# One core of Trainium2: the step products of a linear-attention layer, with s split 1 + 3 groups instead of 2 + 2

## The reference

```
for i in range(12):
    q, k, v = split(x @ Wqkv[i].T + bqkv[i])            # 16 heads of 8
    att = (q @ k.T) * scale                              # per head, no softmax
    x = (att @ v) @ Wproj[i].T + bproj[i] + x
x = layernorm(x0 + x)
x = layernorm(x + (silu(x @ wg.T) * (x @ wu.T)) @ wd.T)
```

## Time and profile before

| | |
|---|---|
| median of 3 runs | 310.81 us (310.21 to 310.88) |
| span of the profiled execution | 308.2 us |
| what lies around the span (median less span) | 2.6 us |
| PE busy | 302.1 us, 98% |
| PE weight loads busy | 283.8 us, 92% |
| DVE / ACT / POOL busy | 70% / 62% / 43% |
| mean granted clock of PE | 0.999 of 2.4 GHz |

### The profile page before, as it was taken

How to read it: one execution, slowest core, us unless ns; L and a number is a source line. 1 busy time by engine, 2 the same in 40 slices (tenths; PEclk the granted TensorE clock), 3 DMA queues, 4 the chain that set the end, 5 groups by cost and what they waited for, 6 DMA issues and landing times.

```text
span 308.2 us, 9599 instructions
## 1 busy us (share of the span) xinstructions
PE 302.1 (98%) x4010; PEld 283.8 (92%) x4010; DVE 216.9 (70%) x651; ACT 192.0 (62%) x459; POOL 133.8 (43%) x142
## 2 busy tenths in 40 slices
PE   8999999999999999999999999999999999999994
PEld 8989999899998998989989999899998889999983
DVE  0477586676876768758677587676765997888874
ACT  3458667686585675865758668577586276444451
POOL 3064180480723806418045072360634663655533
PEclk9999999999999999999999999999999999999999
DMA  7603003030030210300203002020000000121112
GB/s 265 265 2 113 6 6 109 4 113 2 2 115 3 74 43 4 113 4 10 105 5 113 2 3 79 4 75 6 5 0 2 2 2 0 37 64 41 34 35 72
DMA packets 8908, 14.96 MB, mean 49 GB/s; under 512 B 800, under 2 KB 5280, under 8 KB 8864
## 3 DMA queue, kind: packets, MB, share of 16 engines
q1 hardware_dynamic: 8144, 13.34, 13.1%
q10 hardware_dynamic: 720, 0.99, 0.9%
HBM read 12.23 MB, written 2.10 MB: 46 GB/s over the span
## 4 chain that ended last, share of the span: by engine, by line
PE 96%; DMA 1%; DVE 1%; POOLq 0%; issue 0%; POOL 0%; ACT 0%; SPq 0%
PE ps L988 14%; PE ps L1097 14%; PE ps L1063 13%; PE ps L1218 7%; PE ps L946 6%; PE ps L945 6%; PE ps L944 6%; PE ps L1027 4%; PE ps L1007 4%; PE ps L1206 4%; PE ps L1207 4%; PE ps L1178 2%; PE ps L1038 2%; PE ps L961 2%; PE ps L1014 2%; PE ps L999 2%
## 5 line engine op out<-in xcount | busy, mean ns | idle before, releaser
L428 POOL TENSOR_TENSOR wq_lo<-w,wq_hi 128x512 fp32r<-128x512 f32 x12 | 15.3, 1279 | 112.7 <-ACT wq_hi L551 112.7
L466 POOL TENSOR_TENSOR step_lo<-step,step_hi 128x512 fp32r<-128x512 f32 (+1 forms) x44 | 48.9, 1144 | 13.4 <-ACT step_hi L574 13.4
L944 PE MATMUL ps<-state_hi,step_hi 128*128 128x258 f32 x154 | 44.4, 288 | 0.0
L946 PE MATMUL ps<-state_hi,step_lo 128*128 128x258 f32 x154 | 43.6, 283 | 0.0
L945 PE MATMUL ps<-state_lo,step_hi 128*128 128x258 f32 x154 | 43.5, 282 | 0.0
L988 PE MATMUL ps<-w,gram 128*128 128x128 f32 x352 | 42.8, 275 | 0.0
L988 PEld LDWEIGHTS ps<-w,gram 128*128 128x128 f32 x352 | 41.9, 192 | 0.6
L547 ACT COPY gk<-ps 128x512 f32<-128x512 f32 x48 | 28.1, 586 | 21.3 <-PE ps L988 21.3
L1097 PE MATMUL ps<-step,gram 128*128 128x128 f32 x320 | 40.6, 281 | 0.0
L574 ACT CAST step_hi<-step 128x512 fp32r<-128x512 f32 (+1 forms) x44 | 24.7, 566 | 24.7 <-DVE step L764 24.7
L1097 PEld LDWEIGHTS ps<-step,gram 128*128 128x128 f32 x320 | 37.3, 192 | 1.3
(11 more groups left out here) (148 smaller groups left out, 671.2 us busy)
## 6 DMA issues: line engine op xcount, KB each, us to landing
w<-weights SPq DMA_DIRECT2D x12, 592.5 KB, 3.8
xchan<-x_chan SPq DMA_DIRECT2D x8, 256.0 KB, 4.0
out<-xchan SPq DMA_DIRECT2D x7, 256.0 KB, 2.3
xt<-x_tok SPq DMA_DIRECT2D x4, 258.0 KB, 5.5
xt<-x_tok ACTq DMA_DIRECT2D x3, 258.0 KB, 5.3
fw_int<-ffn_weights SPq DMA_DIRECT2D x1, 576.0 KB, 5.0
cst<-consts SPq DMA_DIRECT2D x1, 147.5 KB, 6.9
xt<-x_tok SPq DMA_DIRECT2D x1, 129.0 KB, 2.6
```

The lines of the kernel that those rows point to most:

```text
L466: nc.gpsimd.tensor_tensor(step_part(step_lo, g, True), step_part(step, g, True), step_part(step_hi_f, g, True), ALU.subtract).then_inc(ste ...
L944: nc.tensor.matmul(dst, l_hi, r_hi, start=True, stop=False)
L946: return nc.tensor.matmul(dst, l_lo, r_hi, start=False, stop=True)
```

## The change

S and N are no longer cut 2 + 2 but 1 + 3. Group 0's part of s stays f32: N of group 0 is four rounds-of-quads of 128 columns in f32 (`n_first`). The other three groups' s goes through f32r parts with 384 columns (`n_rest`), first all passes that need only s_hi, then the four with s_lo. ACT copies three quads of s_hi and DVE the fourth; DVE makes all four low parts; POOL's `split_quad` is gone. B products move from between S and N to behind N, there is one instead of two (WHOLE = 1), and ACT instead of DVE copies its result. The shift product moves from the middle of H to behind the B product, so `bq_sums` moves ahead of all `add_identity`. These now all wait for the one end of N, and group 0's is cut in two. H goes group by group. Fifteen batches instead of fourteen are split in U. PSUM banks are assigned anew, the three feed-forward ones among them in the same pattern.

```diff
-WHOLE = 2
+WHOLE = 1
...
+REST = (GROUPS - 1) * P
...
# scalar
-                nc.scalar.copy(s_hi[:, 0:2, :], s_banks(1)[:, 0:2, :]).then_inc(s_hi_ready, 1)
-                for b in range(WHOLE):
-                    if not first:
-                        act.wait_ge(b_whole_ready, at(WHOLE, b + 1))
-                    nc.scalar.copy(s_hi[:, 2 + b, :], s_banks(1)[:, 2 + b, :]).then_inc(s_hi_ready, 1)
+                for i in range(QUADS - 1):
+                    nc.scalar.copy(s_hi[:, i, :], ps[:, S_REST.start + i, 0:REST]).then_inc(s_hi_ready, 1)
+                if not first:
+                    act.wait_ge(b_whole_done, at(WHOLE, 0))
+                    nc.scalar.copy(b_whole[:, :, :], ps[:, B_WHOLE_BANK, 0:WHOLE * P].rearrange("p (b c) -> p b c", b=WHOLE))\
+                        .then_inc(b_whole_ready, WHOLE)
...
# vector
+                    dve.wait_ge(s_done, at(2, 2))
+                    nc.vector.tensor_copy(s_hi[:, QUADS - 1, :], ps[:, S_REST.stop - 1, 0:REST]).then_inc(s_hi_last_ready, 1)
...
-                low_of_s(0)
-                low_of_s(2)
+                for i in range(QUADS):
+                    low_of_s(i)
...
-                add_identity(0)
-                add_identity(1)
-                if not last:
-                    bq_sums()
-                if not last:
-                    add_identity(2)
-                    add_identity(3)
...
+                bq_sums()
+                add_identity(0, range(0, 2))
+                add_identity(0, range(2, GB))
                 if last:
-                    add_identity(2)
                     take_shift()
                     nu_columns()
+                    add_identity(1)
                     a_part(0)
+                    add_identity(2)
                     add_identity(3)
                     return
+                add_identity(1)
+                take_shift()
+                add_identity(2)
+                add_identity(3)
...
# tensor
+                def n_first():
+                    for i in range(QUADS):
+                        if i % 2 == 0:
+                            pe.wait_ge((s_low_half_ready, s_high_half_ready)[i // 2], at(1, 1))
+                        if i == 0:
+                            pe.wait_ge(s_high_half_ready, at(1, 1))
+                        for k in range(QUADS):
+                            r = slice(QUAD * k, QUAD * (k + 1))
+                            nc.tensor.matmul(ps[:, N_BANKS.start + k, 0:P], w[r, s, WQ + P * i:WQ + P * (i + 1)], s_rows[r, i, :],
+                                             start=i == 0, stop=i == QUADS - 1)
+                def n_rest():
+                    def one_pass(left, right, i, first_pass=False, last_pass=False):
+                        for k in range(QUADS):
+                            r = slice(QUAD * k, QUAD * (k + 1))
+                            done = nc.tensor.matmul(ps[:, N_BANKS.start + k, P:P + REST], left[r, P * i:P * (i + 1)], right[r, i, :],
+                                                    start=first_pass, stop=last_pass)
+                        return done
+                    for i in range(QUADS):
+                        if i < QUADS - 1:
+                            pe.wait_ge(s_hi_ready, at(QUADS - 1, i + 1))
                         else:
+                            pe.wait_ge(s_hi_last_ready, at(1, 1))
+                        one_pass(wq_hi, s_hi, i, first_pass=i == 0)
+                        if i == 0:
+                            pe.wait_ge(wq_lo_ready, at(1, 1))
+                        one_pass(wq_lo, s_hi, i)
+                    for i in range(QUADS):
+                        pe.wait_ge(s_lo_ready, at(QUADS, i + 1))
+                        done = one_pass(wq_hi, s_lo, i, last_pass=i == QUADS - 1)
+                    done.then_inc(n_done, 1)
...
-                s_stage(0)
-                s_stage(1)
+                s_stage((0,), S_FIRST, 1)
+                s_stage((1, 2, 3), S_REST, GROUPS)
+                if last_layer:
+                    low_parts()
+                n_first()
+                n_rest()
                 if not first:
                     b_whole_stage()
-                if last_layer:
-                    low_parts()
-                n_stage(0)
-                n_stage(1)
+                shift_stage(s, at(1, 1))
...
```

More of the change, by code:

```diff
@@ L132, in build @@
         step_hi_f = step_hi[:].bitcast(F32)
[L134 to L138, removed]
+        s_rows = sb("s_rows", [P, QUADS, P])
+        s_hi = sb("s_hi", [P, QUADS, REST], F32R)
+        s_lo = sb("s_lo", [P, QUADS, REST], F32R)
         wq_hi = sb("wq_hi", [P, QUADS * P], F32R)
@@ L320, in b_whole_out, with splits @@
         def b_whole_out(b):
[L321 to L328, removed]
+            return ps[:, B_WHOLE_BANK, P * b:P * (b + 1)]
+        def splits(e):
+            return min(2, SPLIT - 2 * e)
         def split_group(tile, g):
@@ L594, in layer @@
                     nc.scalar.copy(gram[:, 2 * e:2 * e + 2, :], ps[:, two, 0:P]).then_inc(gram_ready, 1)
-                    if e < SPLIT_PAIRS:
-                        nc.scalar.copy(state_hi[:, 2 * e:2 * e + 2, S_B:S_B + P], ps[:, two, P:2 * P]).then_inc(b_hi_ready, 1)
+                    nc.scalar.copy(state_hi[:, 2 * e:2 * e + splits(e), S_B:S_B + P],
+                                   ps[:, two.start:two.start + splits(e), S_B:S_B + P]).then_inc(b_hi_ready, 1)
             every_layer(layer)
@@ L770, in layer @@
                 take_s()
-                if not first:
-                    for b in range(WHOLE):
-                        dve.wait_ge(b_whole_done, at(WHOLE, b + 1) - WHOLE)
-                        nc.vector.tensor_copy(b_whole[:, b, :], b_whole_out(b)).then_inc(b_whole_ready, 1)
-                low_of_s(0)
-                low_of_s(2)
+                for i in range(QUADS):
+                    low_of_s(i)
                 def bq_sums():
@@ L1015, in rows_stage, with s_stage @@
                         .then_inc(mean_done, 1)
-                def s_stage(h):
-                    for j in range(2):
-                        pe.wait_ge(m_ready, at(GROUPS, GROUPS if h else j + 1))
+                def s_stage(groups, banks, takes):
+                    pe.wait_ge(m_ready, at(GROUPS, takes))
+                    for g in groups:
                         for i in range(QUADS):
                             r = slice(QUAD * i, QUAD * (i + 1))
-                            place = GB * (2 * h + j)
-                            last = nc.tensor.matmul(s_banks(h)[:, i, P * j:P * (j + 1)],
-                                                    mt[r, place:place + QUADS, :].rearrange("p b i -> p (b i)"),
+                            place = P * (g - groups[0])
+                            last = nc.tensor.matmul(ps[:, banks.start + i, place:place + P],
+                                                    group(mt, g)[r].rearrange("p b i -> p (b i)"),
                                                     wp_cent[r, :] if last_layer else w[r, s, WP:WP + P],
```

172 lines of the change are left out of this document (67 added, 105 removed).

## The result

| | before | after |
|---|---|---|
| median | 310.51 us (310.13 to 310.88, 4 runs) | 312.0 us (311.1 to 312.43, 4 runs) |
| span of the profiled execution | 308.19 | 309.21 |
| start of S in the first layer, and in the last | 17.04, 236.89 | 17.10, 236.72 |
| last matmul starts | 303.35 | 303.57 |
| from there to the end of the span | 4.84 | 5.65 |

The ratio after to before is 1.0042 (95% interval 1.0023 to 1.0061): slower, by 1.3 us. 311.5 was forecast with a range of 309.4 to 313.4. The table shows already that the forecast was right for a reason that it doesn't name: the last matmul comes only 0.22 us later, and 0.81 us of the 1.02 in the spans arise behind it, where the prediction had said that nothing changes.

A forecast was written before the change was run, and what follows sets the result against it. PE bounds the kernel (96% of the last chain), with seams and waits deciding. Terms -0.3 + 0.1 + 0.8 + 0.15 = +0.75 take the span from 308.2 to 308.9, the median from 310.8 to 311.5 us; range 309.4 to 313.4.

The forecast's parts named there:

- first layer: The first layer has no B product to lose and still pays for U's additional split batch: +0.1 us.
- ten layers, without conversions: Ten layers at -0.03 us each: U starts 0.17 earlier, one more split batch costs 0.14; -0.3 us in all.
- conversions in layers 1 and 2: ACT's conversions lose their covering wait, so `step_high` and H's parts reach U late: +0.8 us for both, bounds 0 and 1.4.
- last layer up to the bias rows: The last add follows three others and `a_part(0)`, so L1160 starts 8.70 behind S instead of 8.52: +0.15 us.
- 0.22 of waiting for `mt` and 0.08 of refill: In S, groups 1 to 3 wait for all four DVE masks; six rounds start at 0.55, the first paying refill.
- The wait ahead of H: H waits for DVE's add of the first two batches, starting at 5.11 us, 0.20 behind the shift product.
- the saving of 0.17 for U: In each ordinary layer U was to start 8.71 us behind the start of S instead of 8.88.
- The rival of cheaper seams: Refill behind short waits isn't paid, saving 0.08 in S and 0.10 at H per layer: -2.1, 309.4 us; chance 0.27.
- The rival that gave it 0.3 to 0.4 us a layer: DVE's s_lo instructions don't overlap, delaying s_lo, sums and adds in twelve layers: up to 315.9, half strength 313.4; chance 0.22.
- The rival of a falling clock: Short PE idle times let its clock oscillate; one layer at 1.2 GHz costs up to 20 us; chance under 0.01.
- Behind that nothing but bank numbers changes: After the last layer's delay, the rest of the kernel to its end was to change by nothing.
- The 2.6 us around the span: Time added around the profiled span of 308.2 us, with the median of 310.8, to forecast 311.5.

## Why the prediction was right in its number and wrong in its sum

The span grew by 1.02 us. By stretches, against the forecast terms:

| | forecast | measured |
|---|---|---|
| up to S of the first layer | 0 | +0.06 |
| first layer | +0.1 | +0.02 |
| ten layers, without conversions | -0.3 | -0.98 |
| conversions in layers 1 and 2 | +0.8 | +0.73 |
| last layer up to the bias rows | +0.15 | +0.29 |
| from there to the last matmul | 0 | +0.09 |
| behind the last matmul | 0 | +0.81 |

**Layers.** The order of events was right, and their times to 0.1 us but for one. What was off are small terms. In S I charged 0.22 of waiting for `mt` and 0.08 of refill; the rounds that wait start 0.14 late (t = 0.46, 0.05 behind the last mask) and the next one 0.11 late, 0.06 less in all (N at 1.24, not 1.30). The wait ahead of H came out 0.05 shorter (0.29 from shift to H, not 0.34), H itself 0.03 longer (3.63). So the saving of 0.17 for U became 0.24. That the rounds of 384 columns start at 2.05 and not 2.20 is no gain: group 0's eight f32 rounds start 0.11 apart as forecast, but the first f32r round starts only 0.03 behind the last of them and the next one 0.26 behind it, so that the nine take 1.07 together, as worked out (0.90 + 0.175). The rival of cheaper seams asked for 0.18 a layer in all; 0.07 came, so the truth lay between, nearer to the forecast.

**DVE's chain.** The rival that gave it 0.3 to 0.4 us a layer (4.4 us in its price of 315.9, where twelve times 0.4 would be 4.8) has fallen: its parts overlap (1.95 for four), and with 0.47 us less on DVE nothing moves. The Trainium skill's rule (TensorEngine Tiling (Array Packing), "PSUM Bottleneck"), that evacuation may become the bottleneck of row-tiled matmuls, doesn't decide here; the sums' end and the first add, which waits for PE's last round, meet within 0.05 us, so it is near.

**Conversions.** Right in place and size (0.16 and 0.55 for the two layers), and shown by moving them ahead of the wait.

**Clock.** The rival of a falling clock had no part: from the first layer to PE's last matmul the granted clock is 1.00, so 2.4 GHz, in the trace after as before.

**Last layer.** The 8.70 worked out against 8.52 is 0.18, and was entered in the sum as 0.15. The forecast left out an instruction that the change moves: PE's load of the flag now stands between S and N, not ahead of a product that hides it, and N starts 0.30 later. With it behind the shift product, the bias rows start at 8.67, where 8.70 was worked out. DVE then does two adds in a row ahead of the first z, and the feed-forward block starts 0.23 later than before (251.28 against 251.04).

**The end.** The step that failed is "Behind that nothing but bank numbers changes", the term that was put at nothing. The change takes 59 matmul instructions and their weight loads out of PE's program, and so moves where its 16-KB fetches fall. Ahead of the end, the jump over the Else branch fetches its target, as I read the packets: the first comes 1.0 us behind the branch's start and 0.5 us ahead of the last matmul, the branch ends 1.4 us behind the packet's end, and 0.8 us later comes a second packet, which meets the last stores. In the kernel before, a regular fetch lay 1.6 us ahead of the last matmul, the branch ended 1.5 us earlier and the second packet was gone when the stores began. The Trainium skill has the first half of this (Runtime: NRT & Kernel Launch, "Instruction fetch mechanics"): a taken branch to a target outside the two pages at hand waits until a DMA has brought it. The traces agree, with 3.3 to 4.0 us for the branch in all nine other traces that have the jump, and 2.4 in the kernel before; in all ten it ends 1.2 to 1.4 us behind the end of a packet. PE itself isn't late by it, as it has nothing left to do; the last store is.

What remains open: why a regular fetch 1.6 us ahead of the last matmul shortens the branch, as its target lies behind the whole Else variant. The traces narrow it: there too the branch ends 1.4 us behind the end of that packet, which started 0.13 us ahead of the branch instead of 1.0 behind it, and the jump brings one packet and not two. That the place decides is shown only by moving the regular fetch away (2.39 to 3.50 in the same kernel); I didn't manage to bring the short branch about in the changed kernel.

The sum of the body, +0.2, was 0.5 below the forecast, and the end, +0.8 in the profiled execution and 1.5 to 1.9 in the medians, was missing from it. Two errors of opposite sign met, so that 311.5 came near 312.0 by luck. The 2.6 us around the span were another: they compare a median with a faster execution's span, where 1.8 to 1.9 is measured; as only the difference was forecast, it did no harm.

## What to carry to other kernels

Where a program ends in a jump, compare the stretch behind the last matmul by itself before you credit or blame an edit of the body: an edit that changes only the count of instructions can shift it by 1 to 2 us, more than the edit is worth. Products that use the whole array are put where they also cover a wait: a B product between S and N costs 0.53 us here, a second one behind N moves H by 0.08 and U by 0.03. Work that an engine does "in its idle time" belongs ahead of the wait that makes the idle time, not behind it.

## What the runs showed of the hardware

- A 16-KB packet of instructions takes 0.9 to 1.8 us. Where one falls into the last stores, one sixteenth of ACT's store comes behind it, and the store takes 2.6 to 3.5 us to land instead of 1.7 to 1.8.
- A taken branch on PE over the Else variant lasted 3.3 to 4.0 us in nine traces and 2.4 in one, the one not taken 0.09.
- An f32r round of four 32-row tiles over 384 columns takes 0.18 us from start to start, 0.12 over 256 columns; f32 rounds over 128 columns start 0.11 apart.
- Leaving row tiles for two full-array instructions and coming back cost 0.31 us beside the instructions' own time.
- 40 f32 matmuls of one column on a 32x32 tile and their 40 weight loads held PE for 1.35 us in both kernels: 0.017 us for each, however small its data.
